# The expert stage of a convolution, state-space and expert network as one block of 288 tokens per expert

## What is computed

```python
def _L3_ffn_ref(x, gate_w, w1, b1, w2, b2):     # x: layer norm of t, 1024 x 512
    gate_probs = jax.nn.softmax(jnp.einsum('bsh,eh->bse', x, gate_w), axis=-1)
    top_v, top_i = jax.lax.top_k(gate_probs, 2)
    comb_w = jnp.einsum('bsk,bske->bse', top_v, jax.nn.one_hot(top_i, 8, dtype=x.dtype))
    for e in range(8):
        h = jax.nn.silu(jnp.einsum('bsh,hf->bsf', x, w1[e]) + b1[e])   # 512 -> 2048
        y = jnp.einsum('bsf,fh->bsh', h, w2[e]) + b2[e]                # 2048 -> 512
        out = out + y * comb_w[..., e:e + 1]
    return out                                   # t = t + out
```

## Time and profile before

| | us |
|---|---|
| median of 3 runs | 1471.44 |
| lowest, highest | 1467.91, 1472.68 |
| span of the profiled execution | 1469.3 |
| TensorE busy (matmul) in that span | 1237.3 (84%) |
| VectorE busy | 1016.8 (69%) |
| ScalarE busy | 761.8 (52%) |
| GpSimd busy | 298.5 (20%) |
| mean granted TensorE clock | 0.912 |

### The profile page before, as it was taken

The page is one execution under the profiler, slowest core; times in us unless marked ns, Lnnn a source line. Parts: engine busy times, 40 slices in busy tenths (PEclk is TensorE's granted clock), DMA queues, the critical chain, the costliest instruction groups (busy, mean ns, idle before and its releaser), DMA issues.

```text
span 1469.3 us, 33539 instructions
## 1 busy us (share of the span) xinstructions
PE 1237.3 (84%) x12366; PEld 848.8 (58%) x12367; DVE 1016.8 (69%) x1663; ACT 761.8 (52%) x1227; POOL 298.5 (20%) x363
## 2 busy tenths in 40 slices
PE   3735799998588999847489999768999999999996
PEld 2205576775466677423345555636677677767674
DVE  3668888888788888869567667475567755476432
ACT  2236577677666767622643424424466655375331
POOL 0121223332222333422000000034111111111111
PEclk9766999999899999979599999658999999999998
DMA  4043000003200000320220000328347564446111
GB/s 147 1 155 123 13 5 5 5 3 115 69 12 6 5 4 4 104 119 11 97 115 0 0 0 0 134 107 254 136 143 250 191 201 136 143 168 219 24 26 22
DMA packets 38129, 120.26 MB, mean 82 GB/s; under 512 B 9960, under 2 KB 14184, under 8 KB 28080
## 3 DMA queue, kind: packets, MB, share of 16 engines
q1 hardware_dynamic: 32416, 107.28, 20.3%
q0 software_dynamic: 5648, 12.13, 4.1%
HBM read 105.61 MB, written 12.76 MB: 81 GB/s over the span
## 4 chain that ended last, share of the span: by engine, by line
PE 47%; DVE 4%; ACT 2%; issue 2%; POOL 0%; POOLq 0%; DVEq 0%; ACTq 0%
PE banks L2349 16%; PE banks L2370 15%; PE banks L1880 7%; PE banks L1910 3%; PE banks L2319 1%; PE banks L2302 1%; PE banks L1936 1%; PE banks L2336 1%; PE banks L1949 1%; ACT ab_wi_hi L1749 1%; PE banks L2295 1%; PE banks L1959 1%; DVE f_qa L1418 0%; PE banks L1933 0%; ACT ab_un L1783 0%
## 5 line engine op out<-in xcount | busy, mean ns | idle before, releaser
L2349 PE MATMUL banks<-eb_x_hi,eb_w_hi 128*128 128x128 f16 x1344 | 228.7, 220 | 4.7 <-DVE eb_w_lo L2229 4.7
L2349 PE MATMUL banks<-eb_x_lo,eb_w_hi 128*128 128x128 f16 x1344 | 228.6, 220 | 0.0
L2349 PE MATMUL banks<-eb_x_hi,eb_w_lo 128*128 128x128 f16 x1344 | 228.6, 220 | 0.0
L1118 PE MATMUL banks<-mb_u_hi,mb_wi_hi 128*128 (+3 forms) x1088 | 190.7, 221 | 12.4 <-ACT mb_ca L845 10.7
L1118 PE MATMUL banks<-mb_u_hi,mb_wi_lo 128*128 (+3 forms) x1088 | 190.4, 221 | 0.0
L1118 PE MATMUL banks<-mb_u_lo,mb_wi_hi 128*128 (+3 forms) x1088 | 190.2, 221 | 0.0
L2229 DVE TENSOR_TENSOR eb_w_lo<-eb_raw,eb_w_hi 128x2048 f32 (+1 forms) x64 | 142.6, 2287 | 23.0 <-ACT eb_w_hi L2235 16.0
L647 DVE SCALAR_TENSOR_TENSOR mb_ca<-mb_xp,mb_par,mb_ca 128x128 f32<-128x128 f32 x384 | 149.5, 451 | 5.2 <-ACT mb_ca L845 3.4
L2349 PEld LDWEIGHTS banks<-eb_x_hi,eb_w_hi 128*128 128x128 f16 x1344 | 132.4, 99 | 7.4 <-issue 5.1
L2349 PEld LDWEIGHTS banks<-eb_x_lo,eb_w_hi 128*128 128x128 f16 x1344 | 132.4, 98 | 2.4
L2349 PEld LDWEIGHTS banks<-eb_x_hi,eb_w_lo 128*128 128x128 f16 x1344 | 132.4, 99 | 0.0
(11 more groups left out here) (441 smaller groups left out, 2842.6 us busy)
## 6 DMA issues: line engine op xcount, KB each, us to landing
eb_raw<-e_w SPq DMA_DIRECT2D x64, 1024.0 KB, 6.0
mb_ring<-m_in_w SPq DMA_DIRECT2D x8, 1072.0 KB, 6.5
ab_raw<-a_in_w SPq DMA_DIRECT2D x4, 1154.0 KB, 9.0
mb_ring<-m_out_w SPq DMA_DIRECT2D x4, 1024.0 KB, 5.3
xcm<-x_cm SPq DMA_DIRECT2D x4, 512.0 KB, 5.1
t_res<-x_tm SPq DMA_DIRECT2D x1, 2048.0 KB, 8.9
t_kept<-t_res SPq DMA_DIRECT2D x8, 256.0 KB, 2.0
mb_wi_hi<-t_kept SPq DMA_DIRECT2D x1, 2048.0 KB, 9.2
```

The costliest lines, as they stand in the source:

```text
L1118: x = e.matmul(ps[0:width, bank, n * P:(n + 1) * P], a[:, k, f:f + width], b[:, k, ds(i * P, P)], start=(k == 0 and m == 0), stop=(k == KD ...
L2349: o = e.matmul(ps[:, j, c * P:(c + 1) * P], a[:, side, k, f * P:(f + 1) * P], b[:, k, :], start=(k == 0 and m == 0), stop=(k == KD - 1 and ...
```

## The change

In the stages ahead of the experts only the zeroed rows differ: three blocks of spare rows instead of one, in `un_rows` and in the output (six transfers where there were three). In `stage_moe`:

- Each expert has one block of CAP = 288 token places, in three row groups of 128, 128 and 32. The program is written out for all eight experts, without branches. An expert with more than 288 tokens gets further blocks in a loop behind it (`overflows`), up to seven turns, which are empty otherwise.
- Both layers hold weights stationary and stream 288 tokens: for each of 16 feature blocks 12 matmuls of layer 1 and 12 of layer 2. Layer 1 runs EX_AHEAD = 3 feature blocks ahead of layer 2. The result then has features in its partitions; TensorE turns it back by row groups (`turn_y`), VectorE scales it, GpSimd scatters it.
- b1 is added by ScalarE in the silu, out of the matmul result. VectorE rounds the silu's result to f16 and takes the rest (`low`). b2 is added by ScalarE when it copies the result out (`evacuate`).
- The gate product is three f16 products. Slots are not sorted through memory: VectorE marks, for each expert, the places of its tokens (8 operations of 128 x 384), and 24 matmuls of 3 columns give row numbers and gates.
- Weights come in 16 half pieces of 128 x 1024 through six buffers; each engine does one in each step, nine ahead.

```diff
+EX_RAWS = 6
+EX_LEAD = 9
+EX_AHEAD = 3
+CAP = 288
+ROWS = ((0, P), (P, P), (2 * P, CAP - 2 * P))
...
+        def low(s_, count, f):
+            e.wait_ge(s_.silu, count + 1)
+            e.tensor_copy(h_hi[:, f % 4, :], hf[:, f % 2, :]).then_inc(s_.upped, 1)
+            e.wait_ge(s_.upped, count + 1)
+            e.tensor_tensor(h_lo[:, f % 4, :], hf[:, f % 2, :], h_hi[:, f % 4, :], ALU.subtract).then_inc(s_.low, 1)
...
+        for c in range(E * EX_FB):
+            low(m_, c, c % EX_FB)
+            s = c - EX_AHEAD
+            if s < 0:
+                continue
+            if EX_LEAD + s < E * EX_N:
+                lower_main(EX_LEAD + s)
+            x, f = divmod(s, EX_FB)
+            if f == 0 and x + 1 < E:
+                mark(m_, lambda i: pm[:, i, x + 1:x + 2])
...
+            if f == 1 and x + 1 < E:
+                list_rows(m_, x + 1, (x + 1) % 3)
+            if f in (2, 3, 4) and x:
+                scale(m_, x - 1, f - 2, (x - 1) % 3)
...
+            if f in (9, 10, 11) and x + 1 < E:
+                lower_x(m_, x + 1, f - 9, (x + 1) % 2)
...
-                e.activation(hb[:, j % 2, :], hb[:, j % 2, :], ACT.Silu).then_inc(silu_done, 1)
-                e.wait_ge(silu_done, s * EX_FG + (j + 1))
-                e.copy(h_hi[:, j, :], hb[:, j % 2, :]).then_inc(hhi_done, 1)
...
+            e.activation(hf[:, f % 2, :], ps[:, 4 + f % 3, 0:CAP], ACT.Silu, bias=bias).then_inc(s_.silu, 1)
...
+                e.activation(yb[:, d, :], ps[:, d, 0:CAP], ACT.Identity, bias=bias(d)).then_inc(s_.yb_done, 1)
...
-                        for m, (a, b) in enumerate(((w_hi, x_hi), (w_hi, x_lo), (w_lo, x_hi))):
-                            o = e.matmul(ps[:, j, c * P:(c + 1) * P], a[:, side, k, f * P:(f + 1) * P], b[:, k, :],
...
-                    for m, (a, b) in enumerate(((h_hi, w_hi), (h_hi, w_lo), (h_lo, w_hi))):
-                        o = e.matmul(ps[:, 5, :], a[:, j, c * P:(c + 1) * P],
...
+        def listing(s_, marked, columns_of):
+            for r in range(len(ROWS)):
+                for i in range(TT):
+                    if r == 0:
+                        e.wait_ge(s_.marked, marked + (i + 1))
+                    x = e.matmul(ps[:, TR, 3 * r:3 * r + 3], marks[:, i, r * P:(r + 1) * P], columns_of(i),
+                                 start=(i == 0), stop=(i == TT - 1))
+            x.then_inc(s_.listed, 1)
...
+                    x = e.matmul(ps[:, 4 + f % 3, 0:CAP], a[:, side, k, f % EX_FB * P:(f % EX_FB + 1) * P], b[:, xb, k, :],
...
+                    x = e.matmul(ps[:, d, 0:CAP], a[:, side, KD + fx // 4, at + d * P:at + (d + 1) * P], b[:, f % 4, :],
...
+        for s in range(E * EX_FB):
+            x, f = divmod(s, EX_FB)
+            if s + EX_AHEAD < E * EX_FB:
+                layer1_main(s + EX_AHEAD)
+            if f == 1 and x + 1 < E:
+                listing(m_, TT * (x + 1), lambda i: tokg[:, i, x + 1, :])
...
+            if f in (9, 10, 11) and x + 1 < E:
...
+                turn_x(m_, x + 1, f - 9)
...
+            layer2(m_, s, s, x % 2, KD * (x - 1) if f == 0 and x else None)
...
+        e.wait_ge(m_.yb_done, KD * E)
+        for r in range(len(ROWS)):
+            turn_y(m_, E - 1, r)
```

More of the change, by code:

```diff
@@ new lines, in mark, with list_rows @@
+        def mark(s_, values):
+            for i in range(TT):
+                e.tensor_scalar(marks[:, i, :], place[:], values(i), None, ALU.is_equal).then_inc(s_.marked, 1)
+        def list_rows(s_, count, slot):
+            e.wait_ge(s_.listed, count + 1)
+            own(e.tensor_copy(found[:], ps[:, TR, 0:3 * len(ROWS)].rearrange("p (r c) -> p r c", r=len(ROWS))))
+            own(e.scalar_tensor_tensor(out=empty[:], in0=found[:, :, 0], scalar=0.0, in1=trash[:], op0=ALU.is_equal, op1=ALU.mult))
+            e.scalar_tensor_tensor(out=gates[:, slot, :], in0=found[:, :, 2], scalar=1.0 / GATE_STEP, in1=found[:, :, 1],
+                                   op0=ALU.mult, op1=ALU.add)
+            e.scalar_tensor_tensor(out=rows[:, slot, :], in0=found[:, :, 0], scalar=-1.0, in1=empty[:], op0=ALU.add, op1=ALU.add)\
+                .then_inc(s_.rows_done, 1)
@@ L2219, in pieces @@
-        def pieces(x, side, i, start):
-            for q in range(EX_RAWS):
-                lower(e, x, side, i * EX_RAWS + q, q)
-        e.wait_ge(plan_done, 1)
-        experts(e, pieces, block)
-    def lower(e, x, side, n, q):
-        e.wait_ge(whi_done, x * EX_PIECES + (n + 1))
-        e.tensor_tensor(w_lo[:, side, n, :], raw[q], w_hi[:, side, n, :], ALU.subtract).then_inc(wlo_done, 1)
-    def upper(e, side, n, q, m):
-        e.wait_ge(raw_in[q], (m + 1 + EX_PIECES // EX_RAWS) * 16)
-        e.copy(w_hi[:, side, n, :], raw[q]).then_inc(whi_done, 1)
@@ L2288, in pe @@
+        overflows(e, block)
     def pe(e):
@@ L2305, in pe @@
+                x.then_inc(logits, 1)
+        e.wait_ge(ones_set, 1)
         e.wait_ge(mask_done, 1)
[L2306 to L2309 removed]
         for i in range(TT):
[L2311 removed]
@@ L2328, in pe @@
-        x.then_inc(listed, 1)
-        bias_rows(range(4, TT))
-        e.sem_inc(y_mm, YMM0)
-        def turn(s):
-            e.wait_ge(xg_in, s * 16 + 16)
+            at = (TT - 1 - i) * E
+            e.matmul(ps[:, 6, 0:TT * E], ones16[:] if i else core.tri16[:], before[:, at:at + TT * E], start=(i == 0), stop=(i == TT - 1))
+        for i in range(TT):
+            x = e.matmul(ps[:, 6, TT * E:TT * E + E], ones16[:], mask16[:, i * E:(i + 1) * E], start=(i == 0), stop=(i == TT - 1))
+        x.then_inc(ranks, 1)
@@ new lines, in turn_x, with layer1 @@
+                x = e.transpose(ps[:, TR, k * P:k * P + n], xg[0:n, r, k * P:(k + 1) * P], core.ident[0:n, 0:n])
+            x.then_inc(s_.turned, 1)
+        def layer1(s_, f, side, xb, free):
+            if free is not None:
+                e.wait_ge(s_.silu, free)
+            for k in range(KD):
+                for n, (a, b) in enumerate(((w_hi, x_hi), (w_lo, x_hi), (w_hi, x_lo))):
+                    x = e.matmul(ps[:, 4 + f % 3, 0:CAP], a[:, side, k, f % EX_FB * P:(f % EX_FB + 1) * P], b[:, xb, k, :],
+                                 start=(k == 0 and n == 0), stop=(k == KD - 1 and n == 2))
+            x.then_inc(s_.h_mm, 1)
```

702 lines of the change are left out of this document (394 added, 308 removed).

## The result

The changed kernel took 1419.6 us (median of 4 runs, 1418.6 to 1421.3), against 1469.9 for the kernel before on the same chip: a ratio of 0.965, 95% interval 0.963 to 0.967. The forecast was 1418.8 us, 1402 to 1440. The profiled execution has a span of 1419.3 us, where before it was 1469.3. So the direction and the size came out as forecast. The trace says how much of that was understood and how much was errors that cancel.

A forecast was written before the change was run, and what follows sets the result against it. TensorE was taken as the only full engine. In the profiled execution, 975.0 + 2.7 + 376.3 + 39.7 + 5.7 + 17.3 = 1416.7 us against 1469.3, 52.6 less; from the median 1471.4 that gives 1418.8 us, range 1402 to 1440.

The forecast's parts named there:

- layer 1 starts: Opening ahead of the expert loop: layer 1 starts at 975 us instead of 986.05, bounds 972 and 981.
- first 48 matmuls slow: Start of the expert loop: the slow first block costs what it cost before, 2.7 us.
- 3072 matmuls: Expert loop on TensorE: 3072 matmuls of 288 columns at 122.5 ns, 376.3 us where it was 452.
- seven list stretches: TensorE between experts: list matmuls wait for VectorE's marks, 2.66 us each, of which 1.95 is waiting, seven times.
- transposes in the loop, 42 sets: TensorE, per expert: tokens 1.12 plus 0.2 waiting, results 1.32 plus 0.37 waiting, seven times.
- clock drops: List stretches: idleness may lower TensorE's clock, 1.9 us a drop; three taken, 5.7 us, bounds 0 and 13.
- end, from the last matmul: Copy out, transposes, scaling and scatters after the last matmul: 17.3 us against 14.0 before.
- The step of VectorE: Loop step: SiLU 0.41, rounding 0.30, all done by 2.92 of 2.94 us, so hidden; 38 us if uncovered.
- the one with every list dropping the clock: Rival, list stretches: every one drops the clock and transpose waits are 0.5 longer each, 1426 to 1440 us; chance 0.15.
- Weights too late: Rival, loop DMA: smaller weight pieces not exceeding 146 GB/s make loading 460 us and the kernel 1503; chance 0.02.
- VectorE as the bound: Rival, loop: VectorE becomes the bound; its sum is 38.2 of 52.7 us an expert, no chance of its own.
- a spacing under the column count: Rival, loop matmuls: spacing at 288 columns falls under its column count, 61 us per 20 ns, time 1358; chance 0.01.

The follow-up runs named there:

- experiments 6 and 7: The changed kernel with 272 tokens a block rather than 288, and with 304: 1397.0 us (ratio 0.949) and 1432.7 us (ratio 0.973).
- experiment 4: The changed kernel with weight load 10 and all later ones issued only when the first expert's third gather has landed: 1416.0 us, ratio 0.963.
- experiment 3: The changed kernel with the copy of `t` to the output issued six weight loads later, behind load 18 rather than 12: 1421.5 us, ratio 0.965.
- experiment 1: The changed kernel with an expert's marks made at the end of the expert before, except those of the first list: 1404.8 us, ratio 0.954.
- experiment 2: The changed kernel with 16 unused matmuls of 288 columns on TensorE ahead of each of the seven lists: 1417.0 us, ratio 0.962.
- Experiment 5: The changed kernel with the float16 activations from a second SiLU pass on ScalarE instead of VectorE's rounding: 1429.6 us, ratio 0.972.
- experiment 10: The changed kernel with transposes of row groups two steps apart (tokens at steps 7, 9, 11; results at 2, 4, 5): 1416.2 us, ratio 0.964.

## Why the prediction was right

This is the sum of the forecast beside what the trace of the changed kernel has in each place. The waits are summed from TensorE's start times, beyond the normal spacing.

| term | forecast | measured |
|---|---|---|
| layer 1 starts | 975.0 | 977.5 |
| first 48 matmuls slow | 2.7 | 1.4 |
| 3072 matmuls | 376.3 | 376.4 |
| seven list stretches | 7 x 2.66 = 18.6 | 16.5 |
| transposes in the loop, 42 sets | 7 x 3.01 = 21.1 | 23.7 |
| clock drops | 3 x 1.9 = 5.7 | 8.1 (five) |
| end, from the last matmul | 17.3 | 15.8 |
| span | 1416.7 | 1419.3 |

- **The matmuls** carried the result. The straight line between 128 and 512 columns gave 122.5 ns, the trace has 122.5, and experiments 6 and 7 confirm the slope on both sides. The first 48 lost 1.4 us here instead of 2.7, and 1.4 to 2.9 us in the other executions.
- **The opening** had the right length and a wrong account. From `eb_rstd` to layer 1 the forecast has 975.0 - 932.75 = 42.2 us and the trace 42.3; the 2.5 us in the table are those by which the stage began later. Inside, two errors cancel. The logits did not stay where they were but came 4.8 us sooner, outside the bound of 3, and the way from them to the row numbers was 1.0 us shorter. From the row numbers to layer 1 it then took 15.3 us where the forecast has 9.5. The gathers took 6.4 to 8.9 us against the 3.5 of the earlier trace rows, and experiment 4 gives 4.3 of those 5.8 us back. The forecast named this danger, the copy of `t` and the weight halves together, but only as its late bound, and put nothing for it into the sum; experiment 3 shows that the weight loads are enough without the copy.
- **The list stretch** has the mechanism that was forecast, waits for marks made at that moment, and experiment 1 takes it away. Its size was a little too large, since marks of 384 columns took 0.23 us (1.84/8) rather than 0.264.
- **The transposes** were 2.6 us too cheap in the loop, nearly all of it at the tokens: their three sets cost 1.64 us (0.44, 0.74, 0.46) where the forecast had 1.32. The third set, of 32 columns, was priced at 0.24, and the wait of the second at 0.2 instead of 0.3. The results' cost 1.74 where it had 1.69.
- **The clock drops** need the idleness, as argued from the earlier trace rows, and experiment 2 shows it. That there were five and not three was a guess between 0 and 7 and stays one: the forecast had no way to say which lists would drop.
- **The end** was 1.5 us too long. The forecast lets the copying out begin behind the last matmul; but the first of the four parts of the result was finished earlier, and ScalarE began to copy it at 1402.64, 0.8 us ahead of the end of the last matmul (1403.5 by its start and the spacing).
- **The step of VectorE.** SiLU took 0.50 us, not 0.41, and the rounding 0.32, not 0.30. A plain step stalls nothing all the same. No layer-2 row of the chain waits for `eb_h_lo`, as forecast.
- **What the forecast did not price** is the alternative to the rounding on VectorE. It treated the move as an added cost that hides, 38 us if it did not. Experiment 5 shows that it pays against the alternative tried there, a second SiLU pass: 10 of the 50 us would be missing with that. The rounding by a copy on ScalarE, as the kernel before has it, was not tried. The saving isn't in the plain steps but in the one chain per step that runs through ScalarE's weight copy to VectorE, where marks and scalings queue.
- The rivals: the one with every list dropping the clock was half true (five of seven) and would have read 1426 from terms that partly did not come. Weights too late, VectorE as the bound and a spacing under the column count all failed to appear.

So the hit within 1 us is partly luck. The misses were +2.5 (the stages ahead), +2.6 and +2.4 on one side and -1.3, -2.1 and -1.5 on the other, 2.6 us in all in the span, and the opening hides one of 5.8 us each way. The column of measured terms adds up to the span.

## What to carry to other kernels

Where the full engine asks another for something, look at what stands ahead of the answer on the answering engine, and on the one before that: half a microsecond on a ScalarE that is busy for 53% of the span cost TensorE 10 us over the kernel. Work that is known long ahead, like the marks, belongs a step earlier than its reader; here that was worth 16 us, because the wait also cost clock. Sum an engine's spacing from the column count, and read the waits at the seams one by one.

## What the runs showed of the hardware

- TensorE's clock fell to the lower level after stretches of about 2.4 us with little but the 24 list matmuls in them. It did so behind five of seven equal lists, the same five in two executions of the changed kernel and five others in experiment 3 and again in experiment 4, behind four in experiment 10, behind two of seven with 272 columns (2.5 us), behind none with 304 (2.2 us), and behind three in experiment 5, where the stretches were longer (3.1 us). So the length of a pause alone does not decide; what else does stays open here. With the pause filled, no list was followed by a drop.
- A drop cost 1.3 to 1.7 us each time: for 12 to 15 matmuls the spacing was 240 ns instead of 122.
- The three gathers of the opening, of 128, 128 and 32 rows, took 3.6, 4.1 and 3.4 us by themselves and 6.4, 8.9 and 7.5 us beside three weight loads of 512 KB and the start of the output copy; beside weight loads alone the second took 9.6. Holding the loads back until the gathers had landed made nobody wait for the loads.
- The spacing of matmuls with a new weight load each was the column count at 2.4 GHz and 2.5 ns at 128, 272, 288, 304 and 512 columns.
